# A one-core decoder layer: order of the first attention groups, head-innermost q and k columns, and stacks copied SBUF to SBUF

## The reference, cut to what matters

```python
# x: (4, 512, 512), ctx: (4, 512, 256); 16 heads of D = 32
q = rope((x @ Wq + bq).reshape(B, S, H, D))     # pairs (2i, 2i+1) of a head are rotated
k = rope((x @ Wk + bk).reshape(B, S, H, D))     # x*cos + (-x_odd, x_even)*sin
v = (x @ Wv + bv).reshape(B, S, H, D)
scores = einsum('bshd,bthd->bhst', q, k) / sqrt(D), causal mask
a = einsum('bhst,bthd->bshd', softmax(scores), v).reshape(B, S, E) @ Wo + bo
x = layernorm(x + a)
x = layernorm(x + cross_attention(x, ctx))
x = layernorm(x + gated_ffn(x))
```

## Time and profile before

| | us |
|---|---|
| median of three executions | 973.81 |
| lowest, highest | 972.51, 975.72 |
| the profiled execution, its own time | 973.03 |
| its span in the profile | 971.2 |
| PE busy | 929.9 (96%) |
| DVE busy | 728.6 (75%) |
| POOL busy | 598.1 (62%) |
| ACT busy | 514.4 (53%) |
| DMA queue q1, share of 16 engines | 36.5% |

### The profile page before, as it was taken

One profiled execution on the slowest core, in us unless ns is written; L12 is line 12 of the kernel. 1 busy time (PEld: TensorE's weight loads), 2 busy tenths in 40 slices (PEclk: granted clock), 3 DMA queues, 4 the chain that ended last, 5 costly groups with the idle time before them and its releaser, 6 DMA issues.

```text
span 971.2 us, 16196 instructions
## 1 busy us (share of the span) xinstructions
PE 929.9 (96%) x5272; PEld 756.6 (78%) x5272; DVE 728.6 (75%) x1589; ACT 514.4 (53%) x1150; POOL 598.1 (62%) x645
## 2 busy tenths in 40 slices
PE   7888999999999978999999999999999999999997
PEld 5666888888887856887778888888878788888885
DVE  5667778778877876779776777777877877767777
ACT  4577777777877776566244433333534263333333
POOL 2467746745865546457468766667846776665644
PEclk9999999999999999999999999999999999999999
DMA  6976666965867770012101201111011023111112
GB/s 222 255 198 169 181 175 170 258 169 141 223 182 200 200 251 1 23 59 103 57 0 66 65 33 66 49 51 65 33 43 56 33 109 109 39 60 65 33 33 87
DMA packets 40883, 105.20 MB, mean 108 GB/s; under 512 B 4960, under 2 KB 5344, under 8 KB 38752
## 3 DMA queue, kind: packets, MB, share of 16 engines
q1 hardware_dynamic: 40800, 104.16, 36.5%
HBM read 78.98 MB, written 25.17 MB: 107 GB/s over the span
## 4 chain that ended last, share of the span: by engine, by line
PE 76%; DVE 8%; ACT 5%; POOL 5%; issue 3%; DMA 3%; SPq 0%; POOLq 0%; DVEq 0%; ACTq 0%
PE pd L711 26%; PE pj L659 15%; PE pj L711 10%; PE pg L711 5%; PE pu L711 5%; PE pv L702 4%; PE ps L674 4%; PE pa L687 2%; PE pb L687 2%; POOL raw L1461 1%; PE pc L687 1%; ACT e L945 1%; DMA qk_scratch<-raw 1%; POOL raw L1466 1%; POOL raw L1470 1%
## 5 line engine op out<-in xcount | busy, mean ns | idle before, releaser
L901 ACT ACTIVATE prob<-prob,nmax 128x512 f32<-128x512 f32 (+3 forms) x256 | 143.8, 562 | 72.9 <-DVE nmax L1165 71.9
L1165 DVE CUSTOM_DVE_ANT_0 prob<-ps,mask 128x512 f32<-128x512 f32 (+3 forms) x256 | 124.1, 487 | 71.9 <-PE ps L674 66.3
L674 PE MATMUL ps<-ks,qs 128*128 128x256 f32 (+2 forms) x256 | 104.9, 412 | 7.1 <-DVE nmax L1165 5.4
L1628 POOL TENSOR_TENSOR g_lo<-gated,g_hi 128x512 fp32r<-128x512 f32 x32 | 49.5, 1548 | 95.3 <-ACT g_hi L1005 95.3
L1298 DVE TENSOR_TENSOR xb<-pd,xb 128x512 f32<-128x512 f32 x116 | 79.4, 685 | 27.4 <-PE pd L711 27.4
L1461 POOL TENSOR_TENSOR raw<-raw,cos 128x512 f32<-128x512 f32 x32 | 42.3, 1322 | 90.6 <-DVE pj L1147 75.1
L1621 POOL TENSOR_TENSOR wop_lo<-wsum,wop_hi 128x512 fp32r<-128x512 f32 x64 | 81.7, 1300 | 1.3 <-ACT wop_hi L990 1.3
L1005 ACT CAST g_hi<-gated 128x512 fp32r<-128x512 f32 x32 | 19.9, 622 | 111.7 <-DVE gated L1358 111.7
L711 PE MATMUL pd<-dn_hi,g_hi 128*128 128x512 f32 x244 | 75.6, 391 | 2.4 <-POOL g_lo L1628 1.1
L711 PE MATMUL pd<-dn_hi,g_lo 128*128 128x512 f32 x244 | 75.1, 389 | 0.0
L711 PE MATMUL pd<-dn_lo,g_hi 128*128 128x512 f32 x244 | 75.1, 389 | 0.0
(11 more groups left out here) (525 smaller groups left out, 2814.4 us busy)
## 6 DMA issues: line engine op xcount, KB each, us to landing
f_raw<-in_w_ffn SPq DMA_DIRECT2D x32, 768.0 KB, 4.2
qs<-qk_scratch SPq DMA_DIRECT2D x64, 256.0 KB, 4.9
ks<-qk_scratch SPq DMA_DIRECT2D x60, 256.0 KB, 7.4
qk_scratch<-qk_hi SPq DMA_DIRECT2D x32, 256.0 KB, 2.1
qk_scratch<-raw SPq DMA_DIRECT2D x32, 256.0 KB, 2.5
res<-in_x SPq DMA_DIRECT2D x4, 1024.0 KB, 5.3
x_scratch<-res SPq DMA_DIRECT2D x4, 1024.0 KB, 6.1
xb<-x_scratch SPq DMA_DIRECT2D x4, 1024.0 KB, 5.9
```

What stands on the lines that cost most here:

```text
L674: pe.matmul(ps[:, t % 2, 0:w], qs[n % 2][:, r, s * P:(s + 1) * P], ks[n % 2][:, r, 0:w], start=True, stop=True).then_inc(s_done, 1)
L901: act.activation(prob[:, t % PROBS, 0:w], prob[:, t % PROBS, 0:w], ACT.Exp, bias=nmax[:, n % 2, i:i + 1], scale=-1.0, accum_out=rsum[:, n ...
L1165: dve.tensor_tensor_reduce(prob[:, t % PROBS, 0:w], ps[:, t % 2, 0:w], mask[:, S - w:S], -D ** -0.5, 3e38, ALU.add, ALU.min, accum_out=nma ...
L1628: pool.tensor_tensor(lo, (gated, gated_b)[b][:], hi.bitcast(F32), ALU.subtract).then_inc((glo_done, glo_b_done)[b], 1)
```

## The change

It touches four things.

1. **Layout.** The q and k columns of a group of four heads are reordered so that the head is the innermost index: partition 4d + r instead of 32r + d. Pair partners are then 4 partitions apart, the cosine and sine tables and the biases follow.
2. **Stacks.** For groups 1 to 15 the store to DRAM is gone. The stack is copied straight from `raw` and `qk_hi` (128 partitions) into the 32-partition blocks, 8 DMAs of 256 KB a group, at slot 16n - 16 (group 1: q at -4, k at 4). `raw` is free for the next group when the stack has landed (`sources_free`). For group 0 head 0 is copied SBUF to SBUF (8 DMAs of 64 KB), and heads 1 to 3 go through DRAM (4 stores, then 4 reads of 192 KB for q, 4 of 64 KB and 4 of 128 KB for k).
3. **First slots.** v2 and v3 move from slots -5 to 2 to slots 0 to 2 and 5 to 7, b from 11 to 15. Group 0's rotation on DVE is one run at slot -21, in the free PSUM banks `pa` and `pb` instead of `swp`. k1's rotation is put off to slots 1 to 3, its split to slots 3 and 4 (`turned`).
4. **Weights and small loads.** w_qk of group 2 is split at -11, w_qk of group 3 at 17 by ACT and DVE (was ACT and POOL at 8), Wo at 18, 20, 22, 24. The loads of Wo, bo and w_qk 3 move from slot -12 to slot 6. Only 128 columns of the mask are loaded, POOL clears the rest. x splits move to 29, 30, 33, 35, and the last x load to 31.

```diff
-SWAP = [i ^ 1 for i in range(32)]
+SWAP = [i ^ 4 for i in range(32)]
-SPLIT_W = {(1, 0): (-22, -20), (2, 0): (-8, -8)}
-SPLIT_LATE = {(3, 0): 8, ("o", 0): 10, ("o", 1): 12, ("o", 2): 14, ("o", 3): 17}
-LOAD_X = (10, 11, 30, 32)
-SPLIT_X = (29, 31, 34, 36)
+SPLIT_W = {(1, 0): (-22, -20), (2, 0): (-11, -11), (3, 0): (17, 17)}
+SPLIT_LATE = {("o", 0): 18, ("o", 1): 20, ("o", 2): 22, ("o", 3): 24}
+LOAD_X = (10, 11, 30, 31)
+SPLIT_X = (29, 30, 33, 35)
...
-    out.append((("b", 0), 11, (1, 1, 1, 1)))
+    out.append((("b", 0), 15, (1, 1, 1, 1)))
...
+    chain += [(("v", 2), 0, (4, 4, 4), 0), (("v", 3), 5, (4, 4, 4), 1)]
...
+def turned(n, u, k):
+    late = (6 if k < SPLIT_QK else 4) if (n, u) == (1, 1) else 0
+    return ENDS["qk"[u], n] + k + late
...
+    def sources_free(eng, u, n):
+        if n == 1:
+            eng.wait_ge((first_q, first_k)[u][0], 64)
+            eng.wait_ge(stored[u], 32)
+        else:
+            eng.wait_ge((q_stacked, k_stacked)[u][(n - 1) % 2], 64 * (n // 2))
...
+        def store(u, lo):
+            sp.wait_ge((qkhi_done, qklo_done)[lo], u + 1)
+            for j in range(4):
+                if lo == (j // 2 if u == 0 else j % 2):
+                    head = raw[0:P:4, u, :] if lo else qk_hi[0:P:4, u, :].bitcast(F32)
+                    sp.dma_start((qs0, ks0)[u][D * j:D * j + D, 0, :].bitcast(F32), head).then_inc((first_q, first_k)[u][0], 16)
+            sp.dma_start(scratch[(2 * lo + u) * P:(2 * lo + u + 1) * P, :], half(u, lo)).then_inc(stored[u], 16)
...
+        def stack(n, u):
+            if n >= 2 and u == 0:
                 sp.wait_ge(s_done, TILES * (n - 1))
+            for lo in range(2):
+                sp.wait_ge((qkhi_done, qklo_done)[lo], 2 * n + u + 1)
                 for j in range(4):
+                    if lo == (j // 2 if u == 0 else j % 2):
+                        sp.dma_start((qs, ks)[u][n % 2][D * j:D * j + D, :, :].bitcast(F32),
+                                     half(u, lo)).then_inc((q_stacked, k_stacked)[u][n % 2], 16)
...
+                    if t == (turned(n, u, SPLIT_QK + 1) if n == 1 else TILES * n - 16) and n:
+                        stack(n, u)
...
-            if t == -12:
+            if t == 6:
+                load_w("o")
+                sp.dma_start(bo[:], d["bo"]).then_inc(bo_in, 16)
                 load_w(3)
-                load_w("o")
...
                 if n:
-                    act.wait_ge(stored[u], 32 * n)
+                    sources_free(act, u, n)
...
+            if t == ENDS["k", 0] + ROTATE:
+                swap(0, 0)
+                times_sin(0, 0)
+                swap(0, 1)
+                first_add(0)
+                times_sin(0, 1)
+                first_add(1)
...
-            if t == -7:
+            if t == 4:
                 spread_bias()
...
+        pool.memset(mask[:, 0:S - P], 0.0).then_inc(mask_done, 1)
```

More of the change, by code:

```diff
@@ L399, in load_x @@
             sp.dma_start(x_raw[:, n % 2, :], d["xT"][n * P:(n + 1) * P, :]).then_inc(x_in[n % 2], 16)
[L401 to L409, removed]
@@ L411, in stack, with half @@
-        def stack(n):
-            if n >= 2:
+        def half(u, lo):
+            return raw[:, u, :] if lo else qk_hi[:, u, :].bitcast(F32)
+        def store(u, lo):
[5 more added lines that the diff above has]
+            sp.dma_start(scratch[(2 * lo + u) * P:(2 * lo + u + 1) * P, :], half(u, lo)).then_inc(stored[u], 16)
@@ new lines, in first_stack @@
+        def first_stack():
+            for u in range(2):
+                sp.wait_ge(stored[u], 32)
+                for r, count in ((1, 3),) if u == 0 else ((1, 1), (2, 2)):
+                    for j in range(4):
+                        rows = (2 * (j // 2 if u == 0 else j % 2) + u) * P
+                        heads = scratch[rows:rows + P, :].rearrange("(d r) s -> d r s", r=4)
+                        sp.dma_start((qs0, ks0)[u][D * j:D * j + D, r:r + count, :].bitcast(F32),
+                                     heads[:, r:r + count, :]).then_inc((first_q, first_k)[u][r], 16)
@@ L468, in finished_rows @@
             sp.dma_start(out[b * P:(b + 1) * P, :], xb[b][:]).then_inc(out_done, 16)
[L470 to L478, removed]
-                                         scratch[rows:rows + P, :].rearrange("(r d) s -> d r s", d=D)).then_inc(first_q, 16)
-                        else:
-                            sp.dma_start(ks0[D * j:D * j + D, r, :].bitcast(F32),
-                                         scratch[rows + D * r:rows + D * r + D, :]).then_inc(first_k[r], 16)
         for u in range(2):
@@ L1131, in first_add @@
             dve.wait_ge(sin_done, u + 1)
-            dve.tensor_tensor(raw[:, u, :], raw[:, u, :], swp[:], ALU.add).then_inc(rot_done, 1)
+            dve.tensor_tensor(raw[:, u, :], raw[:, u, :], swapped(0, u), ALU.add).then_inc(rot_done, 1)
         def split_x(k):
@@ L1409, in _ @@
                 for u in range(2):
-                    if t == ENDS["qk"[u], n] + ROTATE:
+                    if n and t == turned(n, u, ROTATE):
                         swap(n, u)
-                    if t == ENDS["qk"[u], n] + ROTATE + 1:
+                    if n and t == turned(n, u, ROTATE + 1):
                         times_sin(n, u)
-                    if n == 0 and t == ENDS["qk"[u], n] + ADD:
-                        first_add(u)
+            if t == ENDS["k", 0] + ROTATE:
[5 more added lines that the diff above has]
+                first_add(1)
+            for n in range(GROUPS):
                 if t == (TILES * n + NORMALIZE if n < GROUPS - 1 else hop(("r", n), 0) + 3):
@@ L1704, in halves, with by_dim @@
         return w.reshape(P, KT, G, P)
-    angle = pos[None, :] * np.tile(np.repeat(theta, 2), 4)[:, None]
-    sign = np.tile(np.array([-1.0, 1.0], np.float32), P // 2)[:, None]
-    mask = np.zeros((P, S), np.float32)
-    mask[:, S - P:] = np.triu(np.full((P, P), MASKED, np.float32), 1)
+    def by_dim(w):
+        return w.reshape(*w.shape[:-1], 4, D).swapaxes(-1, -2).reshape(w.shape)
+    angle = pos[None, :] * np.repeat(theta, 8)[:, None]
+    sign = np.tile(np.repeat(np.array([-1.0, 1.0], np.float32), 4), D // 2)[:, None]
+    mask = np.triu(np.full((P, P), MASKED, np.float32), 1)
     x = a["x"]
-    qk = np.stack([halves(tiles(a[f"L0_attn_W{n}"])) for n in "qk"])
+    qk = np.stack([by_dim(halves(tiles(a[f"L0_attn_W{n}"]))) for n in "qk"])
     return {
@@ L1717, in layouts @@
         "wo": tiles(a["L0_attn_Wo"]).reshape(P, KT * E),
-        "bcol": np.stack([a[f"L0_attn_b{n}"].reshape(G, P) for n in "qkv"]).transpose(2, 1, 0).reshape(P, 3 * G),
+        "bcol": np.stack([by_dim(a[f"L0_attn_b{n}"].reshape(G, P)) if n in "qk" else a[f"L0_attn_b{n}"].reshape(G, P) for n in "qkv"]).transpose(2, 1, 0).reshape(P, 3 * G),
         "bo": np.broadcast_to(a["L0_attn_bo"], (P, E)),
```

77 lines of the change are left out of this document (35 added, 42 removed).

## The result

The changed kernel takes 1001.47 us (median of 4 runs, 998.79 to 1002.66) beside 973.61 for the kernel before (4 runs, 972.51 to 975.72). The ratio is 1.0279, with a 95% interval from 1.0263 to 1.0296. The forecast was 968.0 with a range up to 972.5, so it was wrong in sign. What came about is the mechanism of rival 4, the hold on `raw` (ACT may not rewrite it until the stack copied from it has landed), with 33.5 us over the forecast where that rival had 13.

What follows compares the result with a forecast made beforehand. PE never waits from group 3 on, so only the first 98 us could give. Cumulative gain: 4.2 us by score 0, 4.9 by score 16, 5.4 by slot 27, then zero; 973.0 - 5.4 = 967.6, 968.4 by median, stated 968.0, range 962.5 to 972.5.

Steps and rivals of the forecast that it cites:

- rival 4: Groups 3 to 15: direct copies landing later than 9.5 us stop ACT at q in 13 groups; 981 us, chance 0.06.
- Groups 3 to 15: Later groups: stacks land before q's next bias step, by 0.3 us in group 7; zero, at most 3 us lost.
- Up to score 0: Start of the kernel: reordered rotation work and earlier q1 bring score 0 to 25.3 us; gain 4.2 us.
- The price of the head copies: Before score 0: k0's last head copies, issued at 21.2 and 21.65, land between 23.7 and 25.1; no PE wait.
- The bank turn before q2: Slots 0 to 15: q2 follows v2 in the same bank, so PE waits for ACT's copy, 0.5 us.
- Slots 0 to 15: Stretch after score 0: 19.3 us of work and 3.4 of waits, score 16 at 48.0; gain so far 4.9 us.
- The thin slots' wait: Slots 11 to 14: only scores and transposes, 2.0 us of PE work in 4.4 us, so 2.4 us of waiting.
- rival 1: Slots 11 to 14: PE idle over half of them, so its clock falls; price 1.7 us, 969.7 us, chance 0.12.
- Slots 16 to 26: Stretch from score 16: 16.4 us of work plus 1.1 waiting for w_lo 3, slot 27 at 65.5; gain 5.4 us.
- Slots 27 to 47: Stretch before group 3, forecast as slots 27 to 42: thin slots and clock fall stay; zero, between -1.5 and +1.5.
- the 5.4 us: Whole front up to slot 27: total gain forecast, slot 27 at 65.5 instead of 70.9 us.
- rival 3: Groups 0 and 1: moved work makes DVE and ACT the bound, slot 27 as late as before; 973.8 us, chance 0.09.

Runs made afterwards that it cites:

- e3: e1 with q stacks copied directly SBUF to SBUF, k stacks still through DRAM: 996.39 us, ratio 1.0228 to the kernel before.
- e1: Changed kernel with its new front and layout, but stacks of groups 1 to 15 through DRAM again: 977.65 us, ratio 1.0043 to the kernel before.
- e6: e1 with k stacks copied directly SBUF to SBUF, q stacks still through DRAM: 977.94 us, ratio 1.0037 to the kernel before.
- e5: e1 with b moved to slots 27 to 30 and PSUM bank 0, its bias spread to slot 26: 974.4 us, ratio 0.9994 to the kernel before.
- e12: e11 with w_qk 3 cast and split in slot 14 instead of 17: 970.87 us, ratio 0.9955 to the kernel before.
- e11: e8 with k1's stores ahead of q1's stack reads on SP, w_qk 3's load between the stacks: 973.4 us, ratio 0.9988 to the kernel before.
- e8: e5 with w_qk 3 loaded right after q1's stores, ahead of q1's stack reads: 974.92 us, ratio 1.0011 to the kernel before.
- e10: e9 with k1's stores ahead of q1's stack reads on SP, w_qk 3's load between the stacks: 973.95 us, ratio 0.9999 to the kernel before.
- e9: e8 with v3 moved to slots 7 to 9 and k2 to slots 11 to 13: 973.77 us, ratio 0.9998 to the kernel before.
- e7: Kernel before with seven sets of 2 MB SBUF-to-SBUF copies appended after its last output, each timed once: 7.5 to 18.5 us a set.
- e4: Kernel before with seven sets of 1 MB copies appended after its last output, each timed once: 4.4 to 11.6 us a set.
- e2: Kernel before with its old front, plus only the new layout and direct stacks of groups 1 to 15: 1037.7 us, ratio 1.0661.

## Why the prediction was wrong, point by point

**Groups 3 to 15: the step that failed.** The prediction took the landing of the direct copies from the reads through DRAM: "The reads took 5.8 us to landing there: 172.5 ... It fits by 0.3 us", and "some 4 us of room" in the other groups. The four kinds of copy took 5.6, 8.5, 10.7 and 13.1 us [the issues above]. In group 7 the q copies were issued between 175.7 and 178.2, and q8's bias step waited 2.98 us, until 186.9. Three things were missed. The term was priced by a row of another kind of transfer, one with DRAM at its far end; rival 4 did name the price from which it would decide, 9.5 us, but the 5.8 was taken as evidence against it, although that row holds no direct copy. The room was put at some 4 us beyond the 5.8, and e3, where waits begin at 8.1, shows some 7.5 from the last issue in all. And the queue was counted in issues and bytes ("8 issues a group instead of 12", "from 3 to 2 MB; hidden, worth nothing"), not in the time for which it is full. Term: 0 predicted; 22.9 us measured in groups 3 to 14 against the kernel before, 279.3 - 257.6 = 21.7 against e1. (The 23.8 between the changed kernel and e1 holds the front's part of the hold too.) In these groups q alone costs 272.7 - 257.6 = 15.1 us (e3), k alone nothing (e6), while the two together cost more than either. With k's copies queued behind q's, k's landing is the longest of the four, 13.1 us, and there most of the waits stand.

**Up to score 0** held in its time: forecast 25.3, measured 25.32. DVE's w_lo took 1.79 us instead of 2.30 (the next one, with POOL idle, took 1.23) and ended at 19.57, where the stepping had 19.75. The price of the head copies was luck in part: the last two went out at 22.57 and 23.13, not at 21.2 and 21.65, and landed in 2.1 us, the lower end of what was assumed, so PE waited 0.17 us. At the upper end, 3.4 us, score 0 would have stood more than 1 us later. The bank turn before q2 also held (0.5 forecast, 0.58 measured).

**Slots 0 to 15** failed by 7.2 us: score 16 came at 55.16, not 48.0. Most of it is the same hold. ACT waited 6.75 us at q2's bias for the stack of q1, and PE 5.90. It hid another wait: in e1, without the hold, score 16 still stands at 54.66, for b's wait of 5.68 us. The prediction had named the hold for groups 3 to 15 and left it out here. q1's raw copies were issued from 31.2 us and took 9.9 us, with the DMA engines full (1.01 in group 0). The thin slots' wait, put at 2.4 us, was 0.78 and 0.47 in the rows. The clock fell too (0.66 from 40 to 50 us), but not as rival 1 said: it was down when PE went on after its stop, at 44.12, and back at full (1.00 from 50 to 60 us) through the thin slots. In e5 it fell after the thin slots, behind waits of 0.78, 0.47, 0.92 and 1.47 us.

**Slots 16 to 26** held: 17.5 forecast, 72.72 - 55.16 = 17.6 measured.

**Slots 27 to 47** were put at zero and cost 5.2 us: group 3 begins 32.4 us after slot 27, where it was 98.22 - 70.94 = 27.3 before. In e1 the same stretch takes 101.62 - 72.46 = 29.2, so 3.3 of the 5.2 us came with the direct stacks: ACT waited there 2.40 us for q3's stack and 0.89 for k3's. The other 1.9 came with the new order and have no cause shown; the waits for x loads, 1.38 and 1.21 us, are no longer than before (1.19 and 1.71).

**The front alone**, had the stacks stayed in DRAM, would not have given the 5.4 us either: e1 is 4.2 us slower than the kernel before. Two causes are shown by taking them away: b read a load of Wo that was not there (e5, 3.2 us by the times, 4.8 by the ratios), and the split of w_qk 3 came late (e12, some 3 us by the ratios). A third is less sure: k1's stores stood behind a wait for q1's landing. Moving them gave some 2 us in e11 beside e8 (ratios 0.9988 and 1.0011, whose intervals meet) and nothing in e10 beside e9. With all three mended, the front is worth 0.45%, or 4.4 us. That is near the 5.4 of the sum, but the way is not the one that was summed: in e12's trace slot 27 stands at 65.31 with the four products of b still to come, and group 3 begins only 0.7 us earlier than before. The sum had taken each late load of the old order as removed ("the Wo and w_qk 3 loads come behind the stacks in the queue") and had not asked when they would then land.

**Rival 4** was worth 13 us in the prediction at 12 us of landing. It had 13 groups at 1 us each; the groups paid 1.9 each, and the front another 12.3 against the forecast, part of which is not the hold. **Rivals 1 and 3** both turned up in part once the hold was taken out. In e5 the clock fell, though later than rival 1 had it, and the time was that of rival 3. Rival 3's reason, DVE and ACT as the bound, is not shown: e12 is faster with the same work on both. They had been given 0.21 together, while rival 4, with no row at all behind its main number, had 0.06.

## What to carry to other kernels

A new kind of transfer has no price in the old trace, however near the bytes; until one has been timed alone, the chance that it holds a buffer too long should be as wide as the unknown. Count a DMA queue by how long it is full (eight copies of 2.3 us in a period of 21), not by issues or bytes, and for each buffer that the copy reads ask who rewrites it, and what is queued behind that on its engine. A gain in the front stays a gain only if the next things due are made earlier as well, so when work is moved up, list the loads and splits that it now meets.

## What the runs showed of the hardware

- Folding 128 SBUF partitions into 32 or 64 takes 18.5 and 17.9 us for 2 MB (e7), where 128 to 128 takes 7.5, 32 to 32 takes 11.6 or 11.8 and 32 to 128 takes 12.2. Through DRAM, the read half of the same stack is faster (6.9 us for 1 MB) than the direct fold (10.2 us, e4).
- A load pays for what is queued ahead of it: 256 KB of x took 3.1 to 3.5 us to landing ahead of the direct copies (the changed kernel) and 12.5 to 13.3 us behind them (e2).
- In the traces SP spends 0.6 us on issuing a direct fold copy and 0.43 us on a read from DRAM (1.26 us for two, 1.71 for four). By e7's rows eight copies between other sets of partitions take 5.1 to 8.6 us to issue.
- The granted clock fell to between 0.50 and 0.54 of full from 50 to 60 us in e5, e8, e9 and e10. From 40 to 50 us PE had been busy for 5.4 to 6.8 us in these. e11 (0.80) and e12 (0.74) had less of the fall. The kernel before and the changed kernel stood at 1.00 from 50 to 60 us, but with other work there, so what the fall costs alone is not separated from the waits.
